# Attention softmax sums: taken from spare columns of the value blocks instead of two products per head pair

## The chip, the cores and the metric

One core of one Trainium2 chip runs the program. The metric is the device time of one execution in microseconds (us). The kernel before took 955.3 us, the median of three runs (955.01 to 956.74). One more execution was taken by the hardware profiler; all rows below come from it.

## What is computed

One block of a gated cross-attention model, all in fp32: 4 sequences ("batches") of 512 tokens with 512 features attend to 64 context tokens with 16 heads of 32 features; then a mixture of 8 experts, 2 for each token, follows. Cut to what matters here:

```
q = ln(x) @ Wq.T + bq ; k, v = ctx @ Wk.T + bk, ctx @ Wv.T + bv
scores = clip(q.k / sqrt(32), -50, 50), masked context tokens at -50
probs  = softmax(scores) ; probs = probs / (sum(probs) + 1e-8)
o      = probs @ v                      # per head, then heads side by side
x      = x + tanh(g0) * layernorm(rs * (o @ Wo.T + bo))
x      = x + tanh(g1) * experts(layernorm(x))
```

The kernel doesn't divide the exponentials before the value product. It multiplies them with the values, sums them, and scales the product by the inverse of the sum.

## The kernel before

**Precision.** Each fp32 operand is split in a high and a low part (`_hi` by ACT, `_lo` = value - high by DVE or GpSimd (POOL)). `product3` (L255) makes a product out of three matmuls: high x high, high x low, low x high.

**Pairs.** The 16 heads of a batch are worked on in 8 pairs `s` = 0 to 7 (m = s // 2, j = s % 2). A pair has a tile of exponentials of 128 rows (two heads x 64 context tokens) by 512 query tokens. ACT makes `ex` and `ex_hi` (`exps`, L1078, or `exp_and_high`, L1053), POOL makes `ex_lo` (`ex_low`, L820), in a ring of four. `clip` (DVE, L465) stands ahead of it, `scores` (PE, L1319) ahead of that.

**Value product.** `pv` (PE, L1333) multiplies the pair's tile with a value block `vbd` of 128 x 128. Of the 128 output rows a pair fills 64; the even pair (j = 0) and the odd pair (j = 1) of one m add up in the same bank 6. `o_copy` (ACT, L1064) copies the full 128 rows to `o_un`, once for two pairs. `pv` also multiplies the same tile, high and low, with a selector `hsel` (L1348 to L1351): two more matmuls of 512 columns into bank 7, which gathers the sums of all 16 heads over the eight pairs.

**Sums.** After pair 7, `copy_sums` (ACT, L1070) copies bank 7 as two halves of 16 rows x 256 columns to `den`. `invert_sums` (DVE, L410) takes the reciprocal of 48 x 256 and splits it in high and low, three instructions in a row. In the next batch `spread` (PE, L1353) brings the inverses to the rows of each head with two matmuls of 256 columns for each m; `normalise` (DVE, L419) multiplies, `o_high` (ACT, L1031) and `o_low` (POOL, L800) split, and `o_product` (PE, L1366) multiplies with Wo. The last batch has its own versions (`last_spread`, L1378, `normalise_half`, `last_o_product`).

**Order.** Nothing is scheduled at run time. Each engine has a hand-written order, in-order queue and semaphores: `batch(b, back, front)` exists for DVE (L472), POOL (L825), ACT (L1077) and PE (L1424). Batch 0 runs without `back` (the back half of the batch before it), batches 1 and 2 are a loop body, batch 3 is written out behind the loop (ACT L1185 to L1206, PE L1527 to L1557). Three stretches of these orders matter below.

- ACT, batch 0: `exps` 4, `exps` 5, `normalise_x(1)` (`hs`, L1003), `exps` 6 and 7, `x_high`, `k_high`, `split_weight(3)`, `q_high(1,0)`, `copy_sums`, `q_high(1,1)`.
- DVE, all batches: `q_low(b+1,0)`, `invert_sums(b)`, `q_low(b+1,1)`, `clip(b+1,0)`, `clip(b+1,1)`, (batch 0: `split_weight(3)`), `v_low(b+1)`, and at the start of the next batch `normalise`.
- PE and ACT at the end of a batch: ACT has `exp_and_high(b+1,0)`, `exp_and_high(b+1,1)`, `h_copy(b-1,2)`, `keep_logits(b-1,1)`; PE's `h_transposes(b-1,3)` (L1402) waits for that `keep_logits`.

Of the kernel before, what the change touches and what calls it, by code (L numbers as in the profile page):

```python
# [4 lines left out]
ALU = mybir.AluOpType  # L5
# [7 lines left out]
P = 128  # L13
# [3 lines left out]
S = 512  # L17
# [23 lines left out]
RING = 4  # L41


def flamingo_gated_block(nc, x, ctx_t, mask, w_attn, b_cols, b_rows, gates, gate_t, w_exp, out):
    st = ExitStack()
    with st:
# [73 lines left out]
        hsel = sb("hsel", [P, P + NH], F32R, pa)  # L120
# [108 lines left out]
        o_l2, last_xb = sem("o_lo_second_half_done"), sem("last_x_with_beta")  # L229
        d_mm, dstats, dmean, dvar, drstd, dgam, xb_done, x1_done = (sem(n) for n in  # L230
# [120 lines left out]
        def _(dve):  # L351
# [58 lines left out]
            def invert_sums(n):  # L410
                dve.wait_ge(den_c, n + 1)
# [4 lines left out]
                dve.tensor_tensor(r_two[2 * LO_ROW:3 * LO_ROW + NH, :], rden[:, :], f32(r_two[0:LO_ROW + NH, :]),  # L416
                                  ALU.subtract).then_inc(r_l, 1)
# [148 lines left out]
            dve.wait_ge(setup, 22)  # L566
# [197 lines left out]
        def _(pool):  # L764
# [5 lines left out]
            for tile in (kbd_hi, kbd_lo, vbd_hi, vbd_lo, hsel, two_rows, bo_two, bsel, r_two):  # L770
# [3 lines left out]
            pool.wait_ge(setup, 14)  # L774

            for g in range(2):
                pool.memset(f32(hsel[g * T:g * T + T, NH - 2 + g:NH - 1 + g]), 1.0).then_inc(setup, 1)

            for i, row in enumerate((0, LO_ROW, 2 * LO_ROW, 3 * LO_ROW)):
                pool.wait_ge(setup, 16 + i)  # L780
                pool.affine_select(out=bsel[row:row + NH, i % 2, :, :, :], in_=ones_s[0:NH, :, :, :],
                                   compare_op=ALU.is_equal,
                                   fill=0.0, base=0, pattern=[[-4, KC], [-1, 4], [0, HD]],
                                   channel_multiplier=1).then_inc(setup, 1)
            for i, row in enumerate((0, LO_ROW)):
                pool.wait_ge(setup, 20 + i)
# [70 lines left out]
            pool.wait_ge(setup, 22)  # L857
# [127 lines left out]
        def _(act):  # L985
# [691 lines left out]
```

## Time and profile before

| | us |
|---|---|
| median of three runs | 955.3 |
| the profiled execution, device time | 956.37 |
| its span from first to last instruction | 954.6 |
| batch 0, value products to the next batch's first | about 46 to 82 |
| batches 1, 2 (loop) | about 82 to 179 |
| batch 3 and the attention's end | about 179 to 244 |
| routing, then experts | about 244 to the end |

A timeline row reads: start in us, duration in us, engine, line, operation, output <- input, shape, count; in square brackets the idle time of the engine ahead of it and who ended it. A matmul's shown duration is not its share of PE's time, since matmuls overlap: what one costs is the distance between the starts of neighbours. Lines of helpers stand for many uses (L259 is `product3`), so the tiles' names tell which use it is.

### The profile page before, as it was taken

Reading aid. Unit: us, or ns where it says so; the run is one execution under the profiler, and the core shown is the slowest. Engines: PE = TensorE matmul, PEld = TensorE weight load, DVE = VectorE, ACT = ScalarE, POOL = GpSimd, SP = SyncE. Lnnn points to the kernel's source line nnn. Section 1 sums busy time; section 2 is a strip of 40 time slices with the busy share of each in tenths; the row PEclk is TensorE's granted clock in tenths of the full one; section 3 lists DMA queues with packets and bytes.
Section 4 is the critical chain, followed back from the end, with each engine's and each line's share of the span. In section 5 each row is a group of like instructions: output and inputs, shape, how many; then the busy total and the mean of one; then the engine's idle time right before and its main releaser. Section 6 shows DMA issues by size and latency. Waiting matters only on the chain.

```text
span 954.6 us, 14632 instructions
## 1 busy us (share of the span) xinstructions
PE 907.7 (95%) x4303; PEld 730.2 (76%) x4304; DVE 431.1 (45%) x802; ACT 383.8 (40%) x740; POOL 268.4 (28%) x330
## 2 busy tenths in 40 slices
PE   8978999987799999999999999999999999999994
PEld 7756777766678888888888888888888888888883
DVE  5658868576781221632632534422542172136111
ACT  4475757544232222622622625322532262235221
POOL 6136555574412112211311311311311221212211
PEclk9999999998699999999999999999999999999998
DMA  8210222106571211541541543611451263121121
GB/s 314 89 45 1 78 99 77 56 34 219 192 279 42 33 22 33 190 129 27 185 140 22 179 151 110 220 22 22 150 180 22 35 203 115 33 33 22 33 33 22
DMA packets 27810, 92.88 MB, mean 97 GB/s; under 512 B 5456, under 2 KB 5456, under 8 KB 21136
## 3 DMA queue, kind: packets, MB, share of 16 engines
q1 hardware_dynamic: 18576, 72.03, 20.3%
q0 software_dynamic: 8640, 20.62, 11.9%
q8 instruction: 8, 0.13, 0.1%
q10 hardware_dynamic: 576, 0.02, 0.0%
q14 instruction: 10, 0.08, 0.0%
HBM read 73.98 MB, written 18.68 MB: 97 GB/s over the span
## 4 chain that ended last, share of the span: by engine, by line
PE 81%; issue 6%; POOL 5%; DVE 3%; ACT 2%; DMA 1%; DVEq 0%; POOLq 0%; ACTq 0%; SPq 0%
PE bank L259 72%; PE bank L1602 3%; POOL ex_lo L822 2%; PE bank L1588 2%; POOL o_lo L802 1%; PE bank L1413 1%; POOL xr L806 1%; PE bank L1407 1%; PE bank L1349 1%; DMA c_raw<-in_ctx_t 1%; PE bank L1301 1%; DMA xg<-h_rows,slot_idx 0%; PE bank L1329 0%; DVE tok_tile L689 0%; DVE xt_lo L386 0%
## 5 line engine op out<-in xcount | busy, mean ns | idle before, releaser
L259 PE MATMUL bank<-g_hi,gt_hi 128*128 128x512 f32 x592 | 237.5, 401 | 0.9 <-DVE gt_lo L715 0.9
L259 PE MATMUL bank<-g_lo,gt_hi 128*128 128x512 f32 x592 | 234.1, 395 | 0.0
L259 PE MATMUL bank<-g_hi,gt_lo 128*128 128x512 f32 x592 | 234.1, 395 | 0.0
L745 DVE TENSOR_TENSOR hid<-silu,bank 128x256 f32<-128x256 f32 x148 | 61.4, 419 | 307.0 <-ACT silu L1266 307.0
L1266 ACT ACTIVATE silu<-bank 128x256 f32<-128x256 f32 x148 | 56.7, 383 | 252.8 <-PE bank L259 252.8
L964 POOL COPY g_idx<-slot_idx 128x1 int32 x37 | 6.9, 186 | 470.1 <-ACT w_nxt L1280 470.1
L259 PEld LDWEIGHTS bank<-g_hi,gt_lo 128*128 128x128 f32 x592 | 111.3, 188 | 26.9
L259 PEld LDWEIGHTS bank<-g_hi,gt_hi 128*128 128x128 f32 x592 | 111.3, 188 | 26.3 <-issue 1.1
L259 PEld LDWEIGHTS bank<-g_lo,gt_hi 128*128 128x128 f32 x592 | 111.4, 188 | 25.0
L259 PE MATMUL bank<-dn_hi,hd_hi 128*128 128x512 f32 x296 | 126.8, 428 | 0.0
L259 PE MATMUL bank<-dn_hi,hd_lo 128*128 128x512 f32 x296 | 116.9, 395 | 0.0
L259 PE MATMUL bank<-dn_lo,hd_hi 128*128 128x512 f32 x296 | 116.4, 393 | 0.0
L613 DVE TENSOR_TENSOR g_lo<-raw,g_hi 128x2048 fp32r<-128x2048 f32 x32 | 72.4, 2285 | 9.8 <-ACT g_hi L1209 9.7
L728 DVE TENSOR_TENSOR hd_lo<-bank,hd_hi 128x256 fp32r<-128x256 f32 x148 | 58.8, 418 | 36.1 <-ACT hd_hi L1249 36.1
L973 POOL DMA_INDIRECT out_rows<-y_sb,s_idx x37 | 59.1, 1598 | 41.5 <-ACT y_sb L1287 35.9
L1249 ACT ACTIVATE hd_hi<-bank 128x256 fp32r<-128x256 f32 x148 | 52.6, 384 | 42.0 <-PE bank L1602 42.0
L259 PEld LDWEIGHTS bank<-dn_hi,hd_lo 128*128 128x128 f32 x296 | 55.9, 189 | 13.8
L259 PEld LDWEIGHTS bank<-dn_lo,hd_hi 128*128 128x128 f32 x296 | 56.1, 189 | 8.1
L822 POOL TENSOR_TENSOR ex_lo<-ex,ex_hi 128x512 fp32r<-128x512 f32 x32 | 43.8, 1388 | 64.8 <-ACT ex_hi L1062 30.3
L259 PEld LDWEIGHTS bank<-dn_hi,hd_hi 128*128 128x128 f32 x296 | 55.8, 189 | 7.8
L1209 ACT ACTIVATE g_hi<-raw 128x2048 fp32r<-128x2048 f32 x32 | 61.0, 1911 | 0.2 <-DMA raw<-in_w_exp 0.2
L944 POOL DMA_INDIRECT xg<-h_rows,g_idx x38 | 50.9, 1339 | 30.7 <-POOL g_idx L964 30.1
(236 smaller groups left out, 1291.3 us busy)
## 6 DMA issues: line engine op xcount, KB each, us to landing
raw<-in_w_exp SPq DMA_DIRECT2D x48, 1024.0 KB, 5.5
xs<-in_x SPq DMA_DIRECT2D x4, 1024.0 KB, 6.7
out_rows<-xr SPq DMA_DIRECT2D x16, 256.0 KB, 2.1
h_rows<-dh SPq DMA_DIRECT2D x16, 256.0 KB, 2.1
raw<-in_w_attn SPq DMA_DIRECT2D x3, 1024.0 KB, 13.9
xr<-in_x SPq DMA_DIRECT2D x3, 1024.0 KB, 6.5
raw<-in_w_attn SPq DMA_DIRECT2D x4, 256.0 KB, 7.3
rows<-in_b_rows SPq DMA_DIRECT2D x1, 1024.0 KB, 17.7
```

Of the source, the lines that this page charges most:

```text
L259: mm = eng.matmul(psum, a(k), b(k), start=(first and k == 0 and j == 0), stop=(last and k == n - 1 and j == 2))
L613: dve.tensor_tensor(dst.rearrange("p k n -> p (k n)"), raw[:, p, :], f32(hi.rearrange("p k n -> p (k n)")), ALU.subtract).then_inc(done, 1)
L728: dve.tensor_tensor(hd_lo[:, 2 * p:2 * p + 2, :].rearrange("p k n -> p (k n)"), bank[4 + p % 2][:, 0:256], f32(hd_hi[:, 2 * p:2 * p + 2, : ...
L745: dve.tensor_tensor(hid[:, p, :], silu[:, p, :], bank[p][:, 256:512], ALU.mult).then_inc(hid_done, 1)
L822: pool.tensor_tensor(ex_lo[:, s % RING, :], ex[:, s % 2, :], f32(ex_hi[:, s % RING, :]), ALU.subtract).then_inc(e_l, 1)
L944: pool.indirect_dma_start(out=xg[:, 0:HW], out_offset=None, in_=h_dram[:, :], in_offset=bass.IndirectOffsetOnAxis(ap=rows, axis=0)).then_i ...
L973: pool.indirect_dma_start(out=out[:, :], out_offset=bass.IndirectOffsetOnAxis(ap=s_idx[:, 0:1], axis=0), in_=y_sb[:, :], in_offset=None, c ...
L1209: act.activation(dst.rearrange("p k n -> p (k n)"), raw[:, p, :], ACT.Copy).then_inc(done, 1)
L1249: act.activation(hd_hi[:, 2 * p:2 * p + 2, :].rearrange("p k n -> p (k n)"), bank[4 + p % 2][:, 0:256], ACT.Copy).then_inc(hd_h, 1)
L1266: act.activation(silu[:, p, :], bank[p][:, 0:256], ACT.Silu).then_inc(silu_done, 1)
L1588: tr = pe.transpose(bank[6][:, k * P:(k + 1) * P], xg[:, k * P:(k + 1) * P], ident[:, :])
L1602: tr = pe.transpose(bank[4 + p % 2][:, c * P:(c + 1) * P], hid[:, p, c * P:(c + 1) * P], ident[:, :])
```

## The change

`hsel` and its two matmuls for each pair are gone. Ones are written once into value blocks at columns the pair does not use: the block for (m, j) has its two ones columns in the 64 output rows that belong to the other pair. So the three matmuls of `product3` give the sums beside the values. Even pairs go to bank 6, odd pairs to bank 7, each its own accumulation, and ACT copies after every pair instead of after two: `pair_copy` first the 8 to 2 rows with sums, then the 64 rows of values. PE's `pv(s)` waits for `pair_copy(s-2)`. `den`, `rden` and `r_two` become 512 columns wide (40 rows instead of 48; `SUMS` is 8), and `spread` takes one matmul of 512 columns for each m. The order of ACT is rewritten around the copies. PE's, DVE's and POOL's orders of steps stay. The setup on POOL has four small memsets for two, and narrower selects.

```diff
-        bsel = sb("bsel", [P, 2, KC, 4, HD], F32R, pa)
-        den = sb("den", [LO_ROW + NH, S // 2], F32, pa)
+        bsel = sb("bsel", [P, KC, 4, HD], F32R, pa)
+        den = sb("den", [LO_ROW + SUMS, S], F32, pa)
...
             def invert_sums(n):
                 dve.wait_ge(den_c, n + 1)
                 dve.reciprocal(rden[:, :], den[:, :]).then_inc(den_r, 1)
                 dve.wait_ge(den_r, n + 1)
-                dve.tensor_scalar(r_two[0:LO_ROW + NH, :], rden[:, :], 1.0, None, ALU.mult).then_inc(r_h, 1)
+                dve.tensor_scalar(r_two[hi, :], rden[:, :], 1.0, None, ALU.mult).then_inc(r_h, 1)
...
+            flat = f32(vbd_hi[:]).rearrange("p m j a d -> p (m j a d)")
+            for j in range(2):
+                for g in range(2):
+                    at = j * P + (1 - j) * T + SUMS - 2 + g
+                    pool.memset(flat[g * T:g * T + T, at:at + 3 * (2 * P - 2) + 1:2 * P - 2], 1.0).then_inc(setup, 1)
...
-            def o_copy(b, m, back):
-                act.wait_ge(pair_mm, b * PAIRS + 2 * m + 2)
-                if back:
+            def pair_copy(b, s, back):
+                m, j = s // 2, s % 2
+                own, free, last = j * T, (1 - j) * T, SUMS - 2 * m
+                act.wait_ge(pair_mm, b * PAIRS + s + 1)
+                if s == 0 and back:
+                    act.wait_ge(den_r, b)
+                sums = act.activation(den[j * LO_ROW:j * LO_ROW + last, :], bank[6 + j][free:free + last, :], ACT.Copy,
+                                      scale=1.0 + 1e-8)
+                if s == PAIRS - 1:
+                    sums.then_inc(den_c, 1)
+                if j == 0 and back:
                     act.wait_ge(o_l, (b - 1) * KC + m + 1)
-                act.activation(o_un[:, m, :], bank[6][:, :], ACT.Copy).then_inc(o_ev, 1)
...
+                act.activation(o_un[own:own + T, m, :], bank[6 + j][own:own + T, :],
+                               ACT.Copy).then_inc(o_ev if j else even_ev, 1)
...
                 if back:
                     for m in range(KC):
                         o_high(b - 1, m)
-                    o_copy(b, 0, back)
...
+                    pair_copy(b, 0, back)
+                    exps(2)
+                    exps(3)
+                    pair_copy(b, 1, back)
+                    pair_copy(b, 2, back)
+                    exps(4)
+                    exps(5)
+                    pair_copy(b, 3, back)
                     normalise_x(b + 1)
+                    pair_copy(b, 4, back)
                     normalise_h(b - 1, 0)
+                    x_high(b + 1, range(0, 2))
+                    normalise_h(b - 1, 1)
+                    pair_copy(b, 5, back)
+                    x_high(b + 1, range(2, KC))
                     exps(6)
                     exps(7)
...
+                else:
+                    exps(2)
+                    pair_copy(b, 0, back)
+                    exps(3)
+                    pair_copy(b, 1, back)
+                    exps(4)
+                    pair_copy(b, 2, back)
+                    exps(5)
+                    pair_copy(b, 3, back)
+                    normalise_x(b + 1)
+                    exps(6)
+                    pair_copy(b, 4, back)
+                    exps(7)
                     x_high(b + 1, range(0, 2))
+                    pair_copy(b, 5, back)
                     x_high(b + 1, range(2, KC))
...
+                pair_copy(b, 6, back)
...
-                copy_sums(b)
-                o_copy(b, 3, back)
+                pair_copy(b, 7, back)
...
                 pe.wait_ge(e_l, b * PAIRS + s + 1)
                 if s == 0:
                     pe.wait_ge(v_l, b * 4 + 4)
-                if j == 0 and (m >= 1 or back):
-                    pe.wait_ge(o_ev, b * KC + m)
-                if s == 0 and back:
-                    pe.wait_ge(den_c, b)
-                product3(pe, bank[6][:, :],
+                if m >= 1 or back:
+                    pe.wait_ge(o_ev if j else even_ev, b * KC + m)
+                product3(pe, bank[6 + j][:, :],
...
-                at = NH - 2 - 2 * s
-                for a, e_ in enumerate((ex_hi, ex_lo)):
-                    mm = pe.matmul(bank[7][:, :], hsel[:, at:at + P], e_[:, s % RING, :],
-                                   start=(s == 0 and a == 0), stop=(s == PAIRS - 1 and a == 1))
-                mm.then_inc(pair_mm, 1)
...
-                for half in range(2):
-                    cols = slice(half * (S // 2), (half + 1) * (S // 2))
-                    mm = pe.matmul(bank[m % 2][:, cols], bsel[:, half, m, :, :].rearrange("p a d -> p (a d)"), r_two[:, :],
-                                   start=True, stop=True)
-                mm.then_inc(r_mm, 1)
+                pe.matmul(bank[m % 2][:, :], bsel[:, m, :, :].rearrange("p a d -> p (a d)"), r_two[:, :],
+                          start=True, stop=True).then_inc(r_mm, 1)
```

`pair_copy(b, 6)` stands behind `split_weight(3)` in batch 0 and behind `h_copy(b-1, 0)` in the loop. In the last batch the order is: copy 0, exponentials 2, copy 1, exponentials 3 and 4, copies 2 and 3, exponentials 5 and 6, copy 4, exponentials 7, copies 5, 6 and 7.

## Rows read from the trace of the kernel before

**Rows 1.** Chain that ended last, 44 to 214 us: shares by line, one piece

```profile
by line: issue 25.8%; PE bank L259 18.3%; POOL ex_lo L822 10.5%; POOL o_lo L802 7.2%; POOL xr L806 4.5%; PE bank L1349 3.4%; POOL o_lo L907 1.9%; ACT hs L1006 1.7%; PE bank L1329 1.6%; POOL rs L810 1.4%; ACT ex L1081 1.4%; PE bank L1413 1.4
...
57.12 2.90 ACT hs L1006 x4
```

**Rows 2.** Stages: length, then busy us of PE, PEld, DVE, ACT, POOL, PEclk, DMA

```profile
44.00:79.00 35.00, 28.77 (x130) 20.39 (x129) 22.57 (x38) 24.70 (x43) 11.80 (x10) 0.95 0.10 31
...
121.00:163.00 42.00, 40.03 (x204) 30.61 (x203) 31.15 (x67) 26.54 (x49) 27.09 (x29) 1.00 0.23 81
```

**Rows 3.** Groups of instructions, 0 to 370 us: busy us, mean ns | idle before

```profile
L1349 PE MATMUL bank<-ex_hi,hsel 128*128 128x512 f32 x32 | 13.1, 409 | 0.0
...
L412 DVE RECIPROCAL rden<-den 48x256 f32<-48x256 f32 x4 | 7.0, 1745 | 6.8 <-ACT den L1073 6.8
...
L1073 ACT ACTIVATE den<-bank 16x256 f32<-16x256 f32 x8 | 3.0, 374 | 5.2 <-PE bank L1349 5.1
```

**Rows 4.** Timeline of PE, batch 2

```profile
137.67 0.50 PE L259 MATMUL bank<-w_hi,o_hi 128*128 128x512 f32 x1 [0.29 <-POOL o_lo L802]
...
158.47 0.50 PE L259 MATMUL bank<-ex_hi,vbd_hi 128*128 128x512 f32 x1 [0.61 <-POOL ex_lo L822]
...
164.50 0.40 PE L1349 MATMUL bank<-ex_hi,hsel 128*128 128x512 f32 x1
164.74 0.39 PE L1349 MATMUL bank<-ex_lo,hsel 128*128 128x512 f32 x1
...
173.39 0.66 PE L1407 MATMUL bank<-ident,dh 128*128 128x128 f32 x4 [0.38 <-ACT logits L1050]
```

**Rows 5.** Timeline of ACT, batch 0

```profile
57.10 2.91 ACT L1006 ACTIVATE hs<-xs,nm_a,rs_a 128x512 f32<-128x512 f32 x4
...
62.29 1.07 ACT L1012 ACTIVATE xt_hi<-bank 128x512 fp32r<-128x512 f32 x2
...
69.43 0.69 ACT L1016 ACTIVATE q_hi<-bank,bcol 128x512 fp32r<-128x512 f32 x1 [0.25 <-PE bank L259]
```

**Rows 6.** Timeline of DVE: bias split, batch 0's end, a short reciprocal

```profile
46.59 0.42 DVE L568 TENSOR_SCALAR bo_two<-rows 1x512 fp32r<-1x512 f32 x1
47.05 0.68 DVE L571 TENSOR_TENSOR bo_two<-rows,bo_two 1x512 fp32r<-1x512 f32 x1
...
71.35 1.75 DVE L412 RECIPROCAL rden<-den 48x256 f32<-48x256 f32 x1 [0.45 <-ACT den L1073]
...
74.01 0.75 DVE L391 SCALAR_TENSOR_TENSOR q_lo<-bank,bcol,q_hi 128x512 fp32r<-128x512 f32 x1
...
248.63 0.25 DVE L660 RECIPROCAL wk<-wden 128x16 f32<-128x16 f32 x1
```

**Rows 7.** Timeline of PE, batch 0 and the start of batch 1

```profile
52.24 0.63 PE L1349 MATMUL bank<-ex_hi,hsel 128*128 128x512 f32 x1
52.67 0.63 PE L1349 MATMUL bank<-ex_lo,hsel 128*128 128x512 f32 x1
...
60.07 1.09 PE L1309 MATMUL bank<-ident,hs 128*128 128x128 f32 x8 [2.30 <-ACT hs L1006]
...
81.62 0.50 PE L259 MATMUL bank<-ex_hi,vbd_hi 128*128 128x512 f32 x1 [1.35 <-DVE vbd_lo L407]
```

**Rows 8.** Timelines of POOL, ACT and DVE, batch 2

```profile
132.58 5.04 POOL L802 TENSOR_TENSOR o_lo<-o_un,o_hi 128x512 fp32r<-128x512 f32 x4 [6.60 <-ACT o_hi L1033]
...
154.23 0.58 ACT L1068 ACTIVATE o_un<-bank 128x512 f32<-128x512 f32 x1
...
165.95 1.75 DVE L412 RECIPROCAL rden<-den 48x256 f32<-48x256 f32 x1 [1.23 <-ACT den L1073]
```

**Rows 9.** Timelines of POOL, DVE and PE, batch 3

```profile
192.74 4.27 POOL L822 TENSOR_TENSOR ex_lo<-ex,ex_hi 128x512 fp32r<-128x512 f32 x3 [0.38 <-ACT ex_hi L1062]
...
201.07 1.75 DVE L412 RECIPROCAL rden<-den 48x256 f32<-48x256 f32 x1 [3.94 <-ACT den L1073]
...
203.65 1.21 PE L1385 MATMUL bank<-r_two,bsel 128*128 128x256 f32 x8
```

More of the change, by code:

```diff
@@ L565, in _ @@
             dve.wait_ge(dset, 5)
-            dve.wait_ge(setup, 22)
+            dve.wait_ge(setup, 23)
             dve.tensor_scalar(bo_two[0:1, :], rows[0:1, 1, :], 1.0, None, ALU.mult).then_inc(bo_done, 1)
@@ L769, in _ @@
             pool.memset(mhalf[:, :], -0.5).then_inc(setup, 1)
-            for tile in (kbd_hi, kbd_lo, vbd_hi, vbd_lo, hsel, two_rows, bo_two, bsel, r_two):
+            for tile in (kbd_hi, kbd_lo, vbd_hi, vbd_lo, two_rows, bo_two, bsel, r_two):
                 pool.memset(f32(tile[:]), 0.0).then_inc(setup, 1)
@@ L773, in _ @@
             pool.memset(den[:, :], 1.0).then_inc(setup, 1)
-            pool.wait_ge(setup, 14)
-            for g in range(2):
-                pool.memset(f32(hsel[g * T:g * T + T, NH - 2 + g:NH - 1 + g]), 1.0).then_inc(setup, 1)
+            pool.wait_ge(setup, 13)
+            flat = f32(vbd_hi[:]).rearrange("p m j a d -> p (m j a d)")
[3 more added lines that the diff above has]
+                    pool.memset(flat[g * T:g * T + T, at:at + 3 * (2 * P - 2) + 1:2 * P - 2], 1.0).then_inc(setup, 1)
             for i, row in enumerate((0, LO_ROW, 2 * LO_ROW, 3 * LO_ROW)):
-                pool.wait_ge(setup, 16 + i)
-                pool.affine_select(out=bsel[row:row + NH, i % 2, :, :, :], in_=ones_s[0:NH, :, :, :],
+                j = i % 2
+                pool.wait_ge(setup, 17 + i)
+                pool.affine_select(out=bsel[row:row + SUMS, :, 2 * j:2 * j + 2, :], in_=ones_s[:, :, :, :],
                                    compare_op=ALU.is_equal,
-                                   fill=0.0, base=0, pattern=[[-4, KC], [-1, 4], [0, HD]],
+                                   fill=0.0, base=2 - SUMS, pattern=[[2, KC], [-1, 2], [0, HD]],
                                    channel_multiplier=1).then_inc(setup, 1)
             for i, row in enumerate((0, LO_ROW)):
-                pool.wait_ge(setup, 20 + i)
+                pool.wait_ge(setup, 21 + i)
                 pool.memset(f32(two_rows[row:row + 1, :]), 1.0).then_inc(setup, 1)
@@ L855, in batch @@
                     ex_low(b + 1, 1)
-            pool.wait_ge(setup, 22)
+            pool.wait_ge(setup, 23)
             ln_inverse(0)
@@ L1125, in batch @@
                     h_copy(b - 1, 0)
+                pair_copy(b, 6, back)
+                if back:
                     normalise_h(b - 1, 2)
@@ L1162, in _ @@
             x_high(0)
-            act.wait_ge(setup, 22)
+            act.wait_ge(setup, 23)
             act.wait_ge(pad_store, 48)
@@ L1359, in spread @@
                     pe.wait_ge(o_nd, n * KC + m - 1)
-                for half in range(2):
-                    cols = slice(half * (S // 2), (half + 1) * (S // 2))
-                    mm = pe.matmul(bank[m % 2][:, cols], bsel[:, half, m, :, :].rearrange("p a d -> p (a d)"), r_two[:, :],
-                                   start=True, stop=True)
-                mm.then_inc(r_mm, 1)
+                pe.matmul(bank[m % 2][:, :], bsel[:, m, :, :].rearrange("p a d -> p (a d)"), r_two[:, :],
+                          start=True, stop=True).then_inc(r_mm, 1)
             def o_product(n, t):
@@ L1382, in last_spread @@
                 for m in range(KC):
-                    for half in range(2):
-                        cols = slice(half * (S // 2), (half + 1) * (S // 2))
-                        mm = pe.matmul(tail_bank[m][:, cols], bsel[:, half, m, :, :].rearrange("p a d -> p (a d)"), r_two[:, :],
-                                       start=True, stop=True)
-                    mm.then_inc(r_mm, 1)
+                    pe.matmul(tail_bank[m][:, :], bsel[:, m, :, :].rearrange("p a d -> p (a d)"), r_two[:, :],
+                              start=True, stop=True).then_inc(r_mm, 1)
             def last_o_product(t):
@@ L1504, in _ @@
             mm.then_inc(kv_mm, 1)
-            pe.wait_ge(setup, 22)
+            pe.wait_ge(setup, 23)
             pe.wait_ge(w_lo_done, 1)
```

54 lines of the change are left out of this document (16 added, 38 removed).

## The prediction, made before the changed kernel ran

> **What bounds the kernel now.** I read four views in this order: the chain that ended last, the busy times by stage, the groups of instructions, the timelines of each engine. The reader should see that two of them disagree. By busy time PE is the bound in the loop: 40.03 of 42 us, at full clock, and in batch 0 it is busy for 28.77 of 35 us [rows 2]. By the chain of waits, PE's products are a small part of 44 to 214 us: 18.3% for all of L259 and 3.4% for the sum products; POOL's `ex_lo`, `o_lo` and `xr`, and ACT's `hs`, are in it too [rows 1]. So PE is full of work, but several points of every batch are set by another engine, and PE waits little there only because its own work comes out as long. Taking work from PE then shows as a longer wait.
>
> **What is removed.** Each pair loses two matmuls. The second of two neighbours starts 0.23 us after the first (164.50, 164.74 [rows 4]; the 409 ns of [rows 3] is a latency, not a distance). 2 x 8 pairs x 4 batches = 64 matmuls x 0.23 = 14.7 us, 3.7 per batch. `spread` goes from 8 matmuls of 256 columns for a batch to 4 of 512; in batch 3 the eight take 1.21 us with the last one's latency [rows 9], and four at 0.23 with a latency of 0.39 behind the last start take 1.08. I count that as 0.
>
> **What is added on ACT.** A copy from a bank takes 0.58 us alone [rows 8] and two in a row 1.07 [rows 5], so each in a run costs 0.49. Whether 64 rows or 8 rows by 512 columns cost less isn't shown; the nearest row from below is 16 x 256 with 0.37 [rows 3], so the bounds are 0.37 and 0.58. I take 0.49, since the cost in these rows follows columns. Per batch: before 4 copies of 0.49 and two of 0.39 (0.37 and the gap), 2.7 us; after 16 of 0.49, 7.8 us. That is +5.1.
>
> **What is added on DVE.** The reciprocal of 256 columns takes 1.745 us, one of 16 columns 0.25 [rows 3, 6]: (1.745 - 0.25) / 240 = 6.2 ns a column, so 512 columns take 3.35. If the cost went by elements instead, 40 x 512 against 48 x 256 would give 2.9, and the lower bound is no growth. The two that follow take 0.42 and 0.68 at 512 columns [rows 6]. The run of three took 2.66 us, from 71.35 to the next instruction's start at 74.01 [rows 6]; it becomes 3.35 + 0.42 + 0.68 and two gaps of some 0.1, 4.6 us: +2.0 (bounds 0 and +2.2).
>
> The Trainium skill, "VectorE: DVE Perf Modes", section "First, the fixed hardware budget", has the reciprocal repeat its divide 8 times; with its clock of 0.96 GHz my estimate from that page is 4.3 us for 512 columns, and the total would be some 3 us later than mine. The row of 256 columns is below that rule (2.1), so I stay with the row.
>
> **Batch 0: +4.0 us.** Shifts are against the trace of before. ACT stops being slack at 57.10, the start of `hs` [rows 5]. Now copies 2 and 3 stand ahead; copy 2 falls in a wait, copy 3 (two instructions, 1.0 us) doesn't: `hs` +1.0. Copy 4 comes between exponentials 6 and 7: `xt_hi` (62.29) +1.9. Copy 5 hides in ACT's wait for the second transposes. They need `xt_lo`, so the next products of PE are +1.9 and the 2 us that PE saves in this batch by then are wait. Copy 6 stands behind the weight split and ahead of `q_high`: 69.43 becomes about 71.95, +2.5. Then copy 7, of which the sums come first. Pair 7 ends on PE at about 71.95, the q bias and the sums' copy end at 73.2, and the reciprocal starts at 73.3 to 73.4 instead of 71.35 [rows 6], +2.0. With +2.0 of its own, the split of q at 74.01 is +4.0. Behind it on DVE stand two clips, the weight split and `vbd_lo` with no gap, and for that PE already waited at 81.62, 1.35 us [rows 7]. So the first value product of batch 1 is +4.0.
>
> **Batches 1 and 2: +1.3 us each.** From the batch's first value product on: pairs 0 and 1 are 0.9 us shorter, but the Wo product at 137.67 waits for the four `o_lo` on POOL (5.04 us from 132.58), which don't move [rows 4, 8]. Gain 0. Later POOL's own run (`ex_lo` 2 and 3, `xr`, the inverse roots) fixes `normalise_h` 0 and 1. The copy behind it at 154.23 [rows 8] is two instructions now, 0.5 longer, so `xt_hi` 2 and 3 and exponentials 6 and 7 are +0.5, and so is pair 6 at 158.47, where PE already waited for `ex_lo` [rows 4]. What PE saved in pairs 2 to 5 (1.8 us) is wait there. Pairs 6 and 7 give 0.9 back: the sums are ready at -0.4, their copy is 512 columns instead of two of 256 (-0.2), and the reciprocal at 165.95 [rows 8] starts at -0.6 or -0.7. +2.0: the split of q, the clips, exponentials 0 and 1, the copy of h and the logits copy behind them on ACT are all +1.3. PE waited 0.38 for that logits copy at 173.39 [rows 4]. So the batch ends +1.3.
>
> **Batch 3: +1.4 us.** Copies 1 to 4 now stand ahead of exponential 7 with 3 to 4 us more, of which ACT's idle time takes about half. The last `ex_lo`, which ended at 197.0 [rows 9], ends at about 198.9; pair 7 starts then, as late as before, but without sum products its sums are read at 199.9. The reciprocal starts at 200.5 instead of 201.07 [rows 9], the run of three ends at 205.1 instead of 203.6, and `last_spread` (203.65 [rows 9]) stood right behind it. DVE is busy without a real gap behind that to the attention's end, so +1.4 stays.
>
> **Hidden.** The setup's four memsets and narrower selects lie ahead of PE's first value projection, which PE reached from its own queue with no wait; cost 0, else some tenths. The experts are untouched. New waits `pv(s)` on copy s-2: the copy stands ahead of `exps` of pairs further on in every order, so they are met by the time that `ex_lo(s)` is; 0.
>
> **Sum.** 4.0 + 2 x 1.3 + 1.4 = +8.0 us. Against the profiled execution of 956.4 that is 964.4; against the median of 955.3, which I forecast, 963.3. A measurement of this kernel can tell about 0.2%, 1.9 us.
>
> **Rivals.** (a) **PE sets the time after all**: if the delays that I add up are covered, each removed matmul shows. Full effect 955.3 - 14.7 = 940.6; with batch 0 kept at 0 it is 944. For it: PE's 40.03 of 42 us. Against: the chain [rows 1]. It decides from the point where ACT's logits copy isn't later than before, that is where the reciprocal's run grows by less than the 0.7 that it starts earlier. A part of it (3 to 12 us of gain) is the likelier form. Chance 0.20. (b) **Nearly even**: the reciprocal doesn't grow with columns. Then batch 0 is +2.0, the loop -0.7 each (its start), batch 3 -0.6: 0.0, so 955.3; with half of the growth 959. Chance 0.12. (c) **The clock falls in batch 0.** PE has 3.7 us less work there in a longer stretch. In the trace PE has dropped once after waits, and neighbours then start 0.43 us apart (52.24, 52.67 [rows 7]) at the lower level, 1.2 GHz, against 0.23 at 2.4. A run of 12 matmuls of the q product at that level costs 12 x 0.20 = 2.4 us, two such runs 4.8: 968. Against: the wait of 2.30 us ahead of 60.07 [rows 7] was followed by products at full distance. Chance 0.13. The Trainium skill, "TensorE: Matmul & The Clock Gate", section "HAM oscillation — how this bites in real kernels", has a clock that falls when waits between products get long; by that rule (c) happens.
>
> **Numbers.** Forecast 0.55, (a) 0.20, (b) 0.12, (c) 0.13. The forecast's own range is 958 to 967 (copies at 0.37 or 0.58 us, some 5 to 8 on a path: -1 to +1; the growth of DVE's run between 1.0 and 2.2: -4 to +1; roundings 1). The range for 8 in 10 reaches down into the mild part of (a) and up through (c): 951 to 969. Faster by over 0.2%: (a) and a little of (b), 0.22. Within: most of (b), 0.10. Slower: 0.68.
>
> **What would show it.** In the profile after: no `hsel`; 64 product matmuls fewer on PE; PE's busy time down by 10 to 15 us but the experts start later; L412 with 40x512 near 3.35 us; 128 short copies on ACT near 0.58; `hs` of batch 0 one us later; first value product of batch 1 at about 85.6; PE's wait for logits near 2 us in the loop and for `ex_lo` of pair 6 near 2.5; a wait of 1.5 us or more for the last spread. Wrong if the reciprocal takes under 2.5 us, if PE's waits stay under 1 us each, or if PEclk falls in the loop.

## The result: 970.6 us, slower by 1.5%

The changed kernel takes 970.63 us, the median of four runs (969.74 to 971.43), beside 955.89 for the kernel before (955.01 to 956.74). The ratio is 1.0146, with a 95% interval of 1.0125 to 1.0168. The forecast was 963.3 with a range of 951 to 969: the sign was right, the size was not, and the time lies above the range. The profiled execution took 970.13, with a span of 968.4 against 954.6.

### The profile page after: what moved, and what is told of

Its sections match the earlier page's. It is cut to its first block, busy times and chain, and to the rows that moved or that the text cites. A ratio compares the mean times of both kernels' runs of the same rounds, so it can differ in the third digit from the quotient of the medians.

```text
span 968.4 us, 14518 instructions
## 1 busy us (share of the span) xinstructions
PE 900.2 (93%) x4223; PEld 718.7 (74%) x4224; DVE 440.0 (45%) x802; ACT 409.0 (42%) x780; POOL 265.8 (27%) x331
## 4 chain that ended last, share of the span: by engine, by line
PE 74%; issue 7%; POOL 6%; DVE 5%; ACT 4%; DMA 1%; DVEq 0%; SPq 0%; POOLq 0%; ACTq 0%
PE bank L260 67%; PE bank L1604 3%; POOL ex_lo L827 2%; PE bank L1590 2%; POOL o_lo L807 1%; DVE rden L414 1%; DMA raw<-in_w_attn 1%; PE bank L1415 1%; ACT den L1075 1%; POOL xr L811 1%; ACT o_un L1081 1%; POOL xs L894 1%; PE bank L1317 0%; DVE xr L436 0%; POOL rs L815 0%
## 5 line engine op out<-in xcount | busy, mean ns | idle before, releaser
L260 PE MATMUL bank<-g_hi,gt_hi 128*128 128x512 f32 x592 | 237.5, 401 | 0.9 <-DVE gt_lo L716 0.9
L260 PE MATMUL bank<-g_lo,gt_hi 128*128 128x512 f32 x592 | 234.1, 395 | 0.0
L260 PE MATMUL bank<-g_hi,gt_lo 128*128 128x512 f32 x592 | 234.1, 395 | 0.0
L260 PEld LDWEIGHTS bank<-g_hi,gt_lo 128*128 128x128 f32 x592 | 111.3, 188 | 27.0
L260 PEld LDWEIGHTS bank<-g_hi,gt_hi 128*128 128x128 f32 x592 | 111.3, 188 | 26.4 <-issue 1.1
L260 PEld LDWEIGHTS bank<-g_lo,gt_hi 128*128 128x128 f32 x592 | 111.4, 188 | 25.0
L260 PE MATMUL bank<-dn_hi,hd_hi 128*128 128x512 f32 x296 | 126.8, 428 | 0.0
L260 PE MATMUL bank<-dn_hi,hd_lo 128*128 128x512 f32 x296 | 116.9, 395 | 0.0
L260 PE MATMUL bank<-dn_lo,hd_hi 128*128 128x512 f32 x296 | 116.4, 393 | 0.0
L260 PEld LDWEIGHTS bank<-dn_hi,hd_lo 128*128 128x128 f32 x296 | 55.9, 189 | 13.8
L260 PEld LDWEIGHTS bank<-dn_lo,hd_hi 128*128 128x128 f32 x296 | 56.0, 189 | 8.1
L260 PEld LDWEIGHTS bank<-dn_hi,hd_hi 128*128 128x128 f32 x296 | 55.8, 189 | 7.8
```

Source lines behind the costliest of these rows:

```text
L260: mm = eng.matmul(psum, a(k), b(k), start=(first and k == 0 and j == 0), stop=(last and k == n - 1 and j == 2))
```

## The profile after

The busy times of the changed kernel, with the number of instructions of each engine:

```profile
PE 900.2 (93%) x4223; PEld 718.7 (74%) x4224; DVE 440.0 (45%) x802; ACT 409.0 (42%) x780; POOL 265.8 (27%) x331
```

The groups of instructions that grew, 0 to 260 us (busy us, mean ns of one | idle before), answering to [rows 3]:

```profile
L414 DVE RECIPROCAL rden<-den 40x512 f32<-40x512 f32 x4 | 13.4, 3343 | 2.4 <-ACT den L1075 2.2
...
L1081 ACT ACTIVATE o_un<-bank 64x512 f32<-64x512 f32 x32 | 19.0, 592 | 0.4
...
L1075 ACT ACTIVATE den<-bank 2x512 f32<-2x512 f32 x8 | 4.7, 589 | 1.2 <-PE bank L260 1.1
...
L1075 ACT ACTIVATE den<-bank 8x512 f32<-8x512 f32 x8 | 4.7, 588 | 0.2
```

The reciprocal takes 3.34 us as forecast (3.35). A copy takes 0.59 us whether it reads 64 rows or 2. The chain of waits from 44 to 230 us, by line, beside [rows 1]:

```profile
by line: issue 29.9%; POOL ex_lo L827 9.2%; POOL o_lo L807 6.3%; PE bank L260 5.6%; DVE rden L414 5.4%; ACT den L1075 4.2%; POOL xr L811 3.9%; ACT o_un L1081 3.3%; ACT ex L1062 2.3%; ACT ex L1088 1.8%; POOL o_lo L912 1.8%; DVE sc L470 1.6%;
```

The products of PE (L260) fall from 18.3% of the chain to 5.6%. The reciprocal (5.4%), the sums' copies (4.2%) and the copies of the values' rows (`o_un`, 3.3%) stand in their place. The stages, in the columns of [rows 2], show a PE that waits more and is granted a lower clock:

```profile
44.00:86.00 42.00, 28.99 (x117) 19.48 (x116) 26.17 (x41) 31.50 (x54) 13.13 (x11) 0.86 0.07 26
...
86.00:131.00 45.00, 39.17 (x182) 28.40 (x182) 37.38 (x73) 34.52 (x61) 25.88 (x29) 0.94 0.23 81
...
131.00:181.00 50.00, 44.79 (x210) 33.59 (x211) 37.42 (x68) 35.17 (x65) 26.38 (x30) 0.93 0.18 65
```

The kernel before had a granted clock of 1.00 in batch 2 [rows 2] and in batch 1 too:

```profile
79.00:121.00 42.00, 38.66 (x190) 28.52 (x188) 35.63 (x71) 25.91 (x47) 26.67 (x30) 1.00 0.14 51
```

Now the same stages of all kernels. A stage ends with the start of a `spread` row: the first one of batch 1, of batch 2 and of batch 3, then the last spread; the tail runs to the first instruction of the router's routing (the first reduction `m<-logits` on DVE). Behind it come the experts. All in us, differences of starts in one profiled execution each, so a stage also carries what differed by chance in that execution:

| kernel | batch 0 | batch 1 | batch 2 | batch 3 | tail | routing starts |
|---|---|---|---|---|---|---|
| before | 79.64 | 50.96 | 48.31 | 24.74 | 40.67 | 244.32 |
| after | 81.92 | 58.47 | 51.49 | 26.78 | 39.01 | 257.67 |
| e1 PE work put back | 82.88 | 59.86 | 51.94 | 27.25 | 40.21 | 262.14 |
| e2 half of the inverse | 82.05 | 52.65 | 48.25 | 26.05 | 39.01 | 248.01 |
| e3 one sums' copy a batch | 80.52 | 54.97 | 52.51 | 25.77 | 40.12 | 253.89 |
| e4 both less | 79.61 | 51.17 | 47.64 | 25.11 | 40.36 | 243.89 |
| e5 before, PE work less | 79.12 | 50.88 | 48.22 | 23.92 | 38.52 | 240.66 |
| e6 before, long inverse | 82.49 | 56.79 | 51.78 | 26.74 | 39.10 | 256.90 |
| e7 after, wait filled | 83.70 | 55.36 | 49.92 | 26.80 | 39.69 | 255.47 |
| e8 after, inverse later | 82.51 | 50.12 | 48.94 | 26.80 | 38.60 | 246.97 |
| e9 before, inverse later | 78.70 | 49.32 | 48.34 | 24.75 | 39.20 | 240.31 |
| e10 before, long inverse later | 82.34 | 49.91 | 48.35 | 26.76 | 39.10 | 246.46 |

The routing starts 13.35 us later in the changed kernel, nearly all of the 13.8 by which the span grew. The experts give nothing back and cost nothing. Batch 1 alone has over half of it, 7.5 us.

What happens there stands in three timelines of the changed kernel around 122 to 135 us (start, duration, what; in brackets the idle time before it and what ended it). DVE:

```profile
122.44 3.35 DVE L414 RECIPROCAL rden<-den 40x512 f32<-40x512 f32 x1 [0.17 <-ACT den L1075]
125.82 0.42 DVE L416 TENSOR_SCALAR r_two<-rden 40x512 fp32r<-40x512 f32 x1
126.27 0.69 DVE L418 TENSOR_TENSOR r_two<-rden,r_two 40x512 fp32r<-40x512 f32 x1
126.99 0.75 DVE L392 SCALAR_TENSOR_TENSOR q_lo<-bank,bcol,q_hi 128x512 fp32r<-128x512 f32 x1
127.66 1.40 DVE L470 TENSOR_SCALAR sc<-bank,lim 128x512 f32<-128x512 f32 x2
```

ACT:

```profile
125.16 1.29 ACT L1033 ACTIVATE vbd_hi<-v_all 64x128 fp32r x4
128.51 0.63 ACT L1062 ACTIVATE ex<-sc 128x512 f32<-128x512 f32 x1 [2.06 <-DVE sc L470]
...
131.05 0.58 ACT L1050 ACTIVATE ht<-bank 128x512 f32<-128x512 f32 x1
131.53 0.17 ACT L1055 ACTIVATE logits<-bank 128x8 f32 x1
```

And PE:

```profile
131.75 0.66 PE L1409 MATMUL bank<-ident,dh 128*128 128x128 f32 x4 [2.08 <-ACT logits L1055]
132.25 1.64 PE L1415 MATMUL bank<-gate_w,ht 128*128 128x8 f32 x8
133.74 0.77 PE L260 MATMUL bank<-xt_hi,w_hi 128*128 128x512 f32 x1
134.31 0.63 PE L260 MATMUL bank<-xt_lo,w_hi 128*128 128x512 f32 x1
134.74 0.63 PE L260 MATMUL bank<-xt_hi,w_lo 128*128 128x512 f32 x1
```

The wait is handed from engine to engine. The reciprocal and its two followers hold the split of q and the clips until 127.66. ACT idles 2.06 us for a clip. The logits copy behind those exponentials ends at 131.7, and PE has waited 2.08 us for it. Then the matmuls start 0.43 us apart, the distance of the lower clock level, 1.2 GHz, where they were 0.23 apart at 2.4 before the wait. They stay so for the whole run of twelve up to 139.00. The clock doesn't fall in the wait itself: it is still 1.00 until 132.25, half a microsecond after PE is back at work. The kernel before waited 0.38 us at the same place of batch 2 [rows 4] and kept its clock in the loop.

## The experiments

Two theories stood against each other from the start: that the removed PE work was wait already, so the added ACT and DVE work set the end, or that one part of the change alone made the loss. A third came up with the trace: the fall of the clock as a cause of its own.

**e1: put PE's work back** into the changed kernel, without the rest of the old scheme.

```diff
                 m, j = s // 2, s % 2
+                if m >= 1 or back:
+                    pe.wait_ge(o_ev if j else even_ev, b * KC + m)
+                for _ in range(2):
+                    pe.matmul(bank[6 + j][:, :], two_rows[:, :], w_hi[:, 0, 0, :], start=True, stop=True)
                 pe.wait_ge(e_l, b * PAIRS + s + 1)
                 if s == 0:
                     pe.wait_ge(v_l, b * 4 + 4)
-                if m >= 1 or back:
-                    pe.wait_ge(o_ev if j else even_ev, b * KC + m)
```

The wait for the free bank moves ahead of the wait for `ex_lo`, since the added matmuls write into that bank.

> The changed kernel, with two matmuls of 512 columns put back ahead of each pair's value product (into the pair's bank, overwritten by the product), so PE has the work that the sum products were, 64 x 0.23 = 14.7 us. Outputs are unchanged. Theory 1 (the removed work is wait now, and the waits let the clock fall): the time does not rise, and falls where the clock was low, to 963 to 968 us from 970.6. Rival (PE's work still sets the time): +14.7, 985 us. Rival (removed work is wait, but the clock has no part in it): 970 to 973 us.

Measured: 974.04 us (973.95 to 974.55), 1.0184 of before (1.0166 to 1.0203), so 3.4 over the changed kernel. All 64 matmuls ran. At full clock they are 64 x 0.23 = 14.7 us, and less than a quarter of it is seen. None of the expectations names this value; the one that the clock recovers with the work (963 to 968) is refuted, for PE still waits 2.08 us at 134.09 and at 187.55, and runs of matmuls 0.43 apart follow both. What is left is weaker than hoped: the removed work was mostly hidden. Of the 4.5 us by which the routing starts later in the profiled execution, 1.2 lie in the tail, where the edit adds nothing and seven matmuls ran 0.43 apart. Where the rest comes from wasn't tracked down.

**e2: only half of the inverse.** The first 256 columns are inverted and split, the others keep what they hold.

```diff
-                dve.reciprocal(rden[:, :], den[:, :]).then_inc(den_r, 1)
+                dve.reciprocal(rden[:, 0:S // 2], den[:, 0:S // 2]).then_inc(den_r, 1)
...
```

The two instructions that split the inverse are halved in the same way.

> The changed kernel with the inverse made for the first 256 columns alone, three instructions of 256 columns instead of 512; the inverses of the other half of the tokens are left out. Takes 2.0 us from each batch's run on DVE. Theory 1: all of it is on the path in batches 0 and 3, and two thirds of it or more in the loop: -6 to -9 us, 962 to 965. Rival (ACT's copies alone make things late, the inverse is hidden): 969 to 971.

**e3: leave out 28 of the 32 copies of sums**; only the last pair of each batch copies its rows.

```diff
-                sums = act.activation(den[j * LO_ROW:j * LO_ROW + last, :], bank[6 + j][free:free + last, :], ACT.Copy,
-                                      scale=1.0 + 1e-8)
                 if s == PAIRS - 1:
-                    sums.then_inc(den_c, 1)
+                    act.activation(den[j * LO_ROW:j * LO_ROW + last, :], bank[6 + j][free:free + last, :], ACT.Copy,
+                                   scale=1.0 + 1e-8).then_inc(den_c, 1)
```

> The changed kernel with the sums' copies of pairs 0 to 6 left out (28 of 32; the inverses are then of ones). Takes 7 x 0.6 = 4.2 us from ACT in each batch. Theory 1: batch 0 gives 2.0 to 2.5 back, the loop 0.5 to 1 each, batch 3 1 to 2: -4 to -7 us, 964 to 967. Rival (ACT has slack, the inverse alone is it): 969 to 971.

**e4: e2 and e3 together.**

> Both of the last two at once: half of the inverse and 28 of 32 sums' copies left out. Theory 1: the added costs are mostly gone, what PE saved begins to show: 948 to 957 us. Rival (the loss comes from the split in two banks and its waits, or from the clock, whatever ACT and DVE do): above 962.

The total times, 923.99, 927.07 and 938.65 us, can't be set beside 970.6, since other values are routed: the experts' loop makes 35, 35 and 36 turns instead of 37, some 18 us each. The groups on POOL show it by the count of one line, in the changed kernel:

```profile
L969 POOL COPY g_idx<-slot_idx 128x1 int32 x37 | 6.9, 185 | 470.2 <-ACT w_nxt L1296 470.2
```

and in e4:

```profile
L969 POOL COPY g_idx<-slot_idx 128x1 int32 x36 | 6.7, 186 | 457.0 <-ACT w_nxt L1295 457.0
```

So these kernels are read at the start of the routing. Against the changed kernel, the half inverse moves it by -9.7 us (257.67 to 248.01), the missing copies by -3.8, both by -13.8. The half inverse gives somewhat more than was expected (-6 to -9), the copies somewhat less (-4 to -7). Both together end at 243.89, where the kernel before stood at 244.32. The split in two banks with its waits, which e4 keeps, therefore isn't a cause of its own. The timeline of DVE in the changed kernel:

```profile
257.67 0.28 DVE L642 TENSOR_REDUCE m<-logits 128x16 f32<-128x128 f32 x1
```

and in e4:

```profile
243.89 0.29 DVE L642 TENSOR_REDUCE m<-logits 128x16 f32<-128x128 f32 x1
```

Batch 1 is back as well, 51.17 against 50.96. So with most of the added ACT and DVE work cut, 14.7 us less PE work gain 0.4 us.

That -9.7 and -3.8 nearly add up to -13.8 is in part chance. The profiled execution of e3 was its slowest (929.57 against a median of 927.07), and its 3.8 is split unevenly over the loop: batch 1 gains 3.5, batch 2 loses 1.0. In batch 1 PE waits for the logits as long as in the changed kernel, and this time no fall follows. The timeline of PE in e3:

```profile
130.03 0.66 PE L1408 MATMUL bank<-ident,dh 128*128 128x128 f32 x4 [2.08 <-ACT logits L1055]
...
131.65 0.39 PE L260 MATMUL bank<-xt_lo,w_hi 128*128 128x512 f32 x1
131.88 0.40 PE L260 MATMUL bank<-xt_hi,w_lo 128*128 128x512 f32 x1
```

In batch 2 the same wait of 2.08 us is followed by eleven matmuls 0.43 apart. So the share of the copies lies between 3.8 and, by the median, some 2.5 us more. Over the whole, the DVE run is still the larger cause. In batch 0 it isn't. The first value product of batch 1 stands at 85.81 in the changed kernel, 84.72 in e2, 84.36 in e3 and 81.58 in e4. Each part alone gives back 1.1 and 1.5, both give back 4.2.

**e5: the kernel before with less PE work.** 56 of the 64 sum products are left out; the last pair's are made from other tiles, with all sums of a batch from them.

```diff
-                product3(pe, bank[6][:, :],
+                mm = product3(pe, bank[6][:, :],
...
-                for a, e_ in enumerate((ex_hi, ex_lo)):
-                    mm = pe.matmul(bank[7][:, :], hsel[:, at:at + P], e_[:, s % RING, :],
-                                   start=(s == 0 and a == 0), stop=(s == PAIRS - 1 and a == 1))
+                if s == PAIRS - 1:
+                    for a, e_ in enumerate((ex_hi, ex_lo)):
+                        mm = pe.matmul(bank[7][:, :], two_rows[0:32, :],
+                                       ones_s[0:32, :, :, :].rearrange("p m a d -> p (m a d)").bitcast(F32R),
+                                       start=(a == 0), stop=(a == 1))
```

> The kernel before with the sum products of pairs 0 to 6 left out (56 of 64; the last pair's two are made with ones, so every inverse is 1). ACT, DVE and the banks are as before. PE has 56 x 0.23 = 12.9 us less to do. Since other outputs change the routing, and with it the number of expert tiles, only the start of the routing in the trace is compared: 244.3 us before. Theory 1 (the saved work turns into waits): 240 to 245. Rival (PE's work sets the time): 231.5.

Measured: 937.17 us with 36 turns of the experts' loop, so again the routing is read. It starts at 240.66, 3.7 us earlier. 56 x 0.23 = 12.9 us of PE work went. Batches 1 and 2 are shorter by 0.1 each, batch 0 by 0.5, batch 3 by 0.8. The tail has 2.1 of the 3.7 us, though no sum product stands in it: most of that is the lower clock in the tail of the kernel before (see below under the end). The profiled execution was also the fastest of the four (934.53 against a median of 937.17), so 3.7 is rather too much. That is the direct measure of what the change removes, all else kept: next to nothing in the loop.

**e6: the kernel before with a long inverse.** One more reciprocal, of 48 x 320 on tiles of its own, stands ahead of the true one. Nothing else of the change is in it.

```diff
                 dve.wait_ge(den_c, n + 1)
+                dve.reciprocal(rden_w[:, 0:S // 2 + 64], den_w[:, 0:S // 2 + 64])
                 dve.reciprocal(rden[:, :], den[:, :]).then_inc(den_r, 1)
...
```

> The kernel before with a second reciprocal of 48 x 320 on spare tiles ahead of the real one, 2.1 us more in a row on DVE in each batch, nothing else; outputs unchanged. Theory 1 (the length of DVE's run is on the path in the kernel before too): batch 0 +2, each loop batch +1.5 to +2, batch 3 +2, so 963 to 964 us, more if the clock falls. Rival (it only hurts together with the other parts): under 959 us.

Measured: 968.66 us (967.2 to 968.99), a ratio of 1.0129 (1.0103 to 1.0156), above the 963 to 964 that were expected without a fall of the clock. e5 has shown what the other half of the change is worth. The timelines of DVE and of PE in e6, the places that answer to the changed kernel's above:

```profile
122.93 2.15 DVE L414 RECIPROCAL rden_w<-den_w 48x320 f32<-48x320 f32 x1 [1.21 <-ACT den L1077]
125.00 1.69 DVE L415 RECIPROCAL rden<-den 48x256 f32<-48x256 f32 x1
```

```profile
132.25 0.66 PE L1411 MATMUL bank<-ident,dh 128*128 128x128 f32 x4 [2.29 <-ACT logits L1054]
...
134.32 0.46 PE L261 MATMUL bank<-xt_hi,w_hi 128*128 128x512 f32 x1
134.58 0.63 PE L261 MATMUL bank<-xt_lo,w_hi 128*128 128x512 f32 x1
```

2.1 us more on DVE per batch, 8.4 in all, cost 13 us, and they bring the same wait of over 2 us on PE and the same fall of the clock behind it. Stage by stage e6 is the changed kernel within 1.7 us. About 1.5 of its batch 0 isn't the edit's: its first 50 us already ran later (PE's first long wait there ended at 50.79, in the kernel before at 49.31). The setup shows where this starts: seven value projections from 18.53 to 21.09 ran at the lower clock in e6, which is 7 x 0.20 = 1.4 us, and at full clock in the kernel before. The timelines of PE in e6 and in the kernel before:

```profile
18.53 0.63 PE L261 MATMUL bank<-wv_hi,c_hi 128*128 128x512 f32 x1
18.96 0.63 PE L261 MATMUL bank<-wv_lo,c_hi 128*128 128x512 f32 x1
```

```profile
18.66 0.40 PE L259 MATMUL bank<-wv_hi,c_hi 128*128 128x512 f32 x1
18.89 0.39 PE L259 MATMUL bank<-wv_lo,c_hi 128*128 128x512 f32 x1
```

e7 and e10 have the same seven, and the same offset. All this lies ahead of the first value product; why the clock fell there in these three and not in the others isn't settled.

**e7: fill PE's wait.** In the changed kernel eight matmuls of 512 columns stand where PE waits for the logits.

```diff
                 if back:
+                    pe.wait_ge(even_ev, b * KC + KC)
+                    for _ in range(8):
+                        pe.matmul(bank[6][:, :], two_rows[:, :], w_hi[:, 0, 0, :], start=True, stop=True)
                     h_transposes(b - 1, 3)
```

> The changed kernel with eight matmuls of 512 columns (1.8 us, into the free bank 6) ahead of the last transposes of h in batches 1 and 2, where PE waits 2.08 us for the logits' copy and the clock falls behind. Theory 2 (the fall of the clock behind that wait costs 3 us in batch 1 and 1.5 in batch 2): 965 to 968 us against 970.6. Rival (the clock falls for what happened earlier): 970 to 972 us.

Measured: 967.36 us (966.23 to 968.26), 1.0118 of before (1.0092 to 1.0145): 3.3 us faster than the changed kernel and inside the 965 to 968 expected, with more work on PE and nothing taken from DVE or ACT. Batch 1 is 3.1 us shorter and batch 2 by 1.6, and no matmuls 0.43 apart follow the filled wait; batch 0, which the edit doesn't touch, was 1.8 longer in this run. So the low clock behind this wait is worth 3 to 5 us of the loss, and it doesn't come when the wait is filled. The wait makes the fall likely, not certain: of eight such waits, two each in the changed kernel, e1, e3 and e6, seven were followed by it, and the one of e3 shown above was not.

**e8: the inverse later on DVE.** In the loop `invert_sums` moves behind `v_low`; in batch 0 the weight split goes ahead of it.

```diff
                 if front:
                     k_low(b + 1)
+                    if not back:
+                        split_weight(3)
                     q_low(b + 1, 0)
-                invert_sums(b)
+                if not back:
+                    invert_sums(b)
                 if front:
                     q_low(b + 1, 1)
                     clip(b + 1, 0)
                     clip(b + 1, 1)
-                if not back:
-                    split_weight(3)
-                if front:
                     v_low(b + 1)
+                if back:
+                    invert_sums(b)
+                if front:
                     q_low(b + 1, 2)
                     q_low(b + 1, 3)
```

> The changed kernel with DVE's order changed: in the loop the inverse stands behind the clips and the value blocks' low part, ahead of the split of q 2, where DVE waited 2.10 us; in batch 0 the weight split stands ahead of the first split of q, where DVE waited 2.96. Nothing is left out, outputs unchanged. Theory 1 (the place of the run on DVE is what costs, not its length): the loop's loss goes with its clock loss, batch 0 gives about 2 back: 959 to 963 us. Rival (the copies on ACT or the waits between banks hold the loop): above 967.

Measured: 960.42 us (958.57 to 962.23, eight runs), 1.005 of before (1.0034 to 1.0065): 10.2 us faster than the changed kernel and inside the 959 to 963 expected. Not one operation is less; the timelines of DVE and of PE in e8:

```profile
123.07 1.40 DVE L470 TENSOR_SCALAR sc<-bank,lim 128x512 f32<-128x512 f32 x2
124.39 1.23 DVE L408 TENSOR_TENSOR vbd_lo<-v_all,vbd_hi 64x128 fp32r<-64x128 f32 x4
125.65 3.34 DVE L414 RECIPROCAL rden<-den 40x512 f32<-40x512 f32 x1
```

```profile
127.17 0.66 PE L1413 MATMUL bank<-ident,dh 128*128 128x128 f32 x4 [0.39 <-ACT logits L1059]
...
128.79 0.39 PE L260 MATMUL bank<-xt_lo,w_hi 128*128 128x512 f32 x1
129.02 0.40 PE L260 MATMUL bank<-xt_hi,w_lo 128*128 128x512 f32 x1
```

The reciprocal still takes 3.34 us, but behind the clips. PE waits 0.39 us for the logits, as before the change, and stays at 2.4 GHz. Batches 1 and 2 take 99.1 us, those of the kernel before 99.3. What is left of the loss is batch 0 (+2.9), where only the weight split went ahead of the inverse, and batch 3 (+2.1), where nothing did, less a shorter tail (-2.1).

**e9: the same order in the kernel before.** The diff is that of e8.

> The kernel before with the same new order on DVE as the last one had (inverse behind the clips and the value blocks' low part in the loop, weight split ahead of the first split of q in batch 0). Outputs unchanged. Theory 1: PE's wait of 0.38 us for the logits goes in two batches, and the run ahead of batch 1's first product is about 1 to 1.4 shorter: 953 to 955 us, the best of all versions. Rival (the order has no slack to give in the kernel before): 955 to 957.

**e10: e6 in the new order.**

> The kernel before with the second reciprocal of 320 columns (2.1 us more of DVE in each batch) and the new order. Theory 1 (in the loop the place of the inverse costs, not its length): the loop's share of that loss goes, with its clock loss; batches 0 and 3 keep theirs: 957 to 961 us, against 968.7 in the old order. Rival (2.1 us more of DVE work is a loss in any place): 965 or more.

Measured: e9 952.44 us (952.1 to 953.52, six runs), a ratio of 0.9967 (0.9955 to 0.998), 3 us less than the kernel before and a little below the 953 to 955 expected; it beats both kernels. Its routing starts at 240.31:

```profile
240.31 0.28 DVE L645 TENSOR_REDUCE m<-logits 128x16 f32<-128x128 f32 x1
```

In the stages 1.5 of its 4.0 us lie in the tail, where the order doesn't differ: again the kernel before's lower clock there.

e10 has 956.8 us (954.76 to 958.17, ten runs), 1.0003 of before (0.9992 to 1.0015), just below the 957 to 961 expected. The extra reciprocals cost 4.4 us over e9, while in the old order they cost 13.3 (968.66 against 955.36). In the table e10's batches 1 and 2 are e9's within 0.6 us; what is left of the price lies in batch 0, with the later start named under e6, and in batch 3.

## Why the prediction was wrong in size

**Right: what limits, and the removed work.** PE's 14.7 us were taken to be wait already. e5 shows 0.1 us of gain in each batch of the loop. Rival (a) falls by it. PE's busy time fell by 7.5 us (907.7 to 900.2) where 10 to 15 were named, in part because a matmul at the lower clock counts 0.63 us instead of 0.39.

**Right: batch 0.** Forecast `hs` +1.0, the split of q +4.0, the first value product of batch 1 at 85.6. The timelines of ACT, DVE and PE in the changed kernel:

```profile
57.92 2.93 ACT L1011 ACTIVATE hs<-xs,nm_a,rs_a 128x512 f32<-128x512 f32 x4
...
64.20 1.06 ACT L1017 ACTIVATE xt_hi<-bank 128x512 fp32r<-128x512 f32 x2
```

```profile
73.71 3.33 DVE L414 RECIPROCAL rden<-den 40x512 f32<-40x512 f32 x1
...
78.25 0.75 DVE L392 SCALAR_TENSOR_TENSOR q_lo<-bank,bcol,q_hi 128x512 fp32r<-128x512 f32 x1
```

```profile
85.81 0.79 PE L260 MATMUL bank<-ex_hi,vbd_hi 128*128 128x512 f32 x1 [3.28 <-DVE vbd_lo L408]
86.41 0.63 PE L260 MATMUL bank<-ex_lo,vbd_hi 128*128 128x512 f32 x1
```

`hs` is +0.8, `xt_hi` +1.9, the reciprocal starts at 73.71 (forecast 73.4), its run of three takes 4.54 us (4.6), and the value product comes at 85.81, +4.2. Following the queues row by row gave this stage to 0.2 us. The sum is better confirmed than its two halves: 2.0 were put on the copies and 2.0 on the longer run of DVE, and cutting either alone gave back 1.5 (e3) and 1.1 (e2). The case that the reciprocal doesn't grow, rival (b), falls too.

**The step that failed: "So the batch ends +1.3", the term "2 x 1.3" of the sum.** Measured from first value product to first value product, batch 1 grew by 5.6 us (49.5 to 55.1) and batch 2 by 3.2: 8.8 where 2.6 stood in the sum. The mechanism of the step was the right one, the inverse's run in front of the split of q and the clips, up to the logits copy; and the forecast named PE's wait of "near 2 us" for it, which came at 2.08. It priced that wait, but not the fall of the clock behind it. In two ways it was short:

- The clock. Rival (c) had the fall of the clock with the right distance, 0.20 us lost per matmul and 2.4 us for a q product, but put it in batch 0 with a chance of 0.13. It came behind the forecast's own waits: in the q product at 134 to 139 us, behind the wait of 3.28 us at 85.81 until about 89.9, and at 187.2 to 189.7 in batch 2. The rival rested on the reading that PE "has dropped once" in the trace of before; the same trace has a second run of slow matmuls at 216 us, shown below. e7, where the wait for the logits is filled, puts 4.7 us of batches 1 and 2 on it (3.1 and 1.6). The profile's "PEclk" tells it: 0.94 and 0.93 in the loop's stages where [rows 2] has 1.00. In batch 0 it is 0.86 against 0.95, but there the q product ran at full distance, and the stage came out as the sum without (c) had it. The text did say that a fall in the loop would make it wrong; the waits and the rival were never put together. The Trainium skill, "TensorE: Matmul & The Clock Gate", section "HAM oscillation — how this bites in real kernels", has the clock fall when waits between products get long; here the trace agrees in kind at 131.75 and 85.81 us, but in the same kernel a wait of 2.17 us at 160.36 was followed by matmuls at full clock, so the rule doesn't tell which wait it will be.
- The copies. Two instructions for a pair were counted as 2 x 0.49 us. In the run they are 0.60 apart, and in batch 0 a pair costs 1.08 to 1.22 rather than 0.98. The timeline of ACT, batch 0, one of the longer ones:

```profile
65.29 0.59 ACT L1075 ACTIVATE den<-bank 4x512 f32<-4x512 f32 x1
65.89 0.59 ACT L1081 ACTIVATE o_un<-bank 64x512 f32<-64x512 f32 x1
66.50 1.08 ACT L1017 ACTIVATE xt_hi<-bank 128x512 fp32r<-128x512 f32 x2
```

The forecast's upper bound was 0.58, so the range nearly covered this. It comes to some 1.3 us of ACT per batch. e3, which takes 28 copies away, gives back 3.8 us over all stages, a part of it in batch 0, where they were in the sum; so they aren't the main part of the miss. (The list of signs has 128 short copies; by the sum's own 16 per batch there are 64, and the groups above show 32 of them for the values and as many for the sums.)

The clock leaves 1.5 of the 6.2 us missing in the loop (6.2 less the 4.7 of e7). The runs don't divide them between the copies, the inverse and the low clock at 86 to 90 us, which e7 left standing. Of the other signs, PE's wait for the `ex_lo` of pair 6 was named near 2.5 us and came at 1.51 and 1.05.

**Batch 3 and the end.** Forecast +1.4, measured +2.0 to the last spread. The tail then came out 1.7 shorter than before, which the forecast left at 0. That comes from the kernel before, whose Wo products there ran at the lower level in the profiled execution; its timeline of PE:

```profile
214.15 0.66 PE L1407 MATMUL bank<-ident,dh 128*128 128x128 f32 x4 [2.49 <-ACT dh L1038]
...
216.37 0.63 PE L259 MATMUL bank<-w_hi,o_hi 128*128 128x512 f32 x1
216.80 0.63 PE L259 MATMUL bank<-w_lo,o_hi 128*128 128x512 f32 x1
```

The changed kernel has no such stretch in its tail, nor have e6, e8, e9 and e10, whose tails are 38.6 to 39.2. e8 has the same wait (2.48 at 218.87) without the fall. Why one met the low clock and the others not isn't settled. Without this the miss would be larger.

**Summed up.** Forecast 4.0 + 2.6 + 1.4 = 8.0. Measured in the same stages 4.2 + 8.8 + 2.0 - 1.7 = 13.3, and the routing starts 13.35 later. The range was too narrow on its upper side, since it held two things apart that can come together: the forecast's own case makes the waits behind which rival (c) has the clock fall.

## What to carry to other kernels

Before an instruction is widened, read what stands behind it in its engine's queue: 2 us of DVE in front of the clips cost 13 us (e6), the same 2 us behind them, where the order allows it in two of four batches, 4.4 (e10). The fix was the order and not the work, and in e9 it was worth 3 us with no change of the computation at all. When a forecast makes a wait on PE as long as these (2.08 to 2.29 us), price the run of matmuls behind it at the lower clock in the same case, not as a rival. What an engine's work is worth can be measured ahead of the change by leaving it out (e5), which here would have shown a gain of 0.2 us in the loop. And when two profiled executions are compared stage by stage, look first for runs of matmuls 0.43 apart: one of seven moved a stage by 1.4 us where no edit was (e6).

## What the runs showed of the hardware

- A copy of 2, 4, 6 or 8 rows x 512 out of a bank takes 0.57 to 0.59 us, like one of 64 rows or of 128 [rows 8]: its cost doesn't follow the rows; 16 x 256 took 0.37 [rows 3]. Copies of one tile in a run were 0.49 apart [rows 5]; those of a pair, to two tiles and from other rows, are 0.60 apart. Which of the two makes the difference wasn't tried.
- The reciprocal: 1.74 us for 40 x 256 (e2), 2.15 for 48 x 320 (e6), 3.34 for 40 x 512. From the first to the last that is 6.3 ns a column; with 48 rows and 256 columns it took the same 1.745 [rows 3] as with 40. The Trainium skill, "VectorE: DVE Perf Modes", section "First, the fixed hardware budget", would have given some 4.3 us for 512 columns as an estimate; the trace disagrees.
- PE's clock fell behind waits of 2.08 us (131.75), 2.29 (e6) and 3.28 us (85.81), and stayed up behind those of 0.39. It fell in a kernel where PE is busy 93% of the span, and a run of twelve matmuls of 512 columns went by at the lower level. The fall can come after the wait: the slow matmuls begin 2.1 us after PE is back at work behind the wait of 2.08 us that ends at 184.75. The length of the wait alone doesn't decide. No fall followed 2.30 us in the kernel before (60.07 [rows 7]), 2.48 in e8 (218.87), 2.08 in e3 (130.03), nor this one in the changed kernel itself:

```profile
160.36 1.09 PE L1325 MATMUL bank<-ident,hs 128*128 128x128 f32 x8 [2.17 <-ACT hs L1011]
```
